# Choosing the tokens of each expert: one-hot products for two experts at once, 64 weights against 128 moving columns

## The reference

```python
n_tok = b * s                                  # 8192
k = n_tok // E                                 # E = 8 experts, 1024 tokens each
logits = xf @ Wr + br
Sm = jax.nn.softmax(logits, axis=-1)
G_t, idx_t = jax.lax.top_k(Sm.T, k)            # every expert takes its k best tokens
...
tokens = xf[idx]
...
mid = jax.nn.silu(jnp.einsum('keh,ehf->kef', tokens, Wu) + bu)
out = jnp.einsum('kef,efh->keh', mid, W_down) + b_down
y = jnp.zeros_like(xf).at[idx].add(G[..., None] * out)
```

## Time and profile before

| | us |
|---|---|
| median of three runs | 4523.12 |
| lowest and highest | 4513.47, 4530.17 |
| the profiled execution's own time | 4521.61 |
| its span in the trace | 4519.9 |
| TensorE busy (matmuls), share of the span | 3914.8, 87% |
| VectorE busy | 3019.1, 67% |
| first layer's `moe_choose`, softmax to `slots` | 78.3 to 178.5 |
| one-hot columns and products in it (L627 to L565) | 142.6 to 177.5 |

### The profile page before, as it was taken

The page is one execution under the profiler, slowest core; times in us unless marked ns, Lnnn a source line. Parts: engine busy times, 40 slices in busy tenths (PEclk is TensorE's granted clock), DMA queues, the critical chain, the costliest instruction groups (busy, mean ns, idle before and its releaser), DMA issues. The chain is left out here.

```text
span 4519.9 us, 137362 instructions
## 1 busy us (share of the span) xinstructions
PE 3914.8 (87%) x58832; PEld 2629.4 (58%) x58832; DVE 3019.1 (67%) x5402; ACT 2324.4 (51%) x3869; POOL 2358.8 (52%) x1536
## 2 busy tenths in 40 slices
PE   4599798999999996389979799699999999997799
PEld 2366454444444435256657444488878788886577
DVE  6411255888888866721156576699889899996575
ACT  2121142677777771112135477677776777773233
POOL 1154444222222224035433355599999999998454
PEclk7799898999999998689989899899999999998899
DMA  7333377655565637233232476633433343342662
GB/s 223 108 56 49 89 235 209 90 96 94 95 101 94 102 76 235 84 92 56 45 86 66 169 257 249 191 97 97 103 97 87 98 103 96 97 106 101 240 226 76
DMA packets 339380, 550.42 MB, mean 122 GB/s; under 512 B 55456, under 2 KB 238912, under 8 KB 338752
## 3 DMA queue, kind: packets, MB, share of 16 engines
q1 hardware_dynamic: 285264, 467.33, 39.0%
q0 software_dynamic: 24576, 34.10, 4.6%
q10 hardware_dynamic: 28912, 40.02, 2.5%
HBM read 335.56 MB, written 212.32 MB: 121 GB/s over the span
## 5 line engine op out<-in xcount | busy, mean ns | idle before, releaser
L2566 POOL TENSOR_TENSOR s_hc<-s_hs,s_ct 128x1024 f32<-128x1024 f32 x512 | 1202.2, 2393 | 64.6 <-DVE s_hs L2541 63.5
L2541 DVE TENSOR_TENSOR_SCAN s_hs<-s_hs,s_psB 128x1024 f32<-128x1024 f32 x512 | 1133.4, 2270 | 118.4 <-PE s_psB L2457 108.6
L2457 PE MATMUL s_psB<-s_diag,s_duT 128*32 128x128 f32 x32768 | 966.5, 274 | 63.4 <-issue 52.8
L2457 PEld LDWEIGHTS s_psB<-s_diag,s_duT 128*32 128x32 f32 x32768 | 925.2, 111 | 148.5 <-issue 116.8
L1380 DVE CUSTOM_DVE_ANT_0 a_masked<-a_psM,k_later 128x1024 f32<-128x1024 f32 (+7 forms) x1024 | 721.3, 750 | 132.7 <-PE a_psM L1439 116.5
L1362 ACT ACTIVATE a_wt<-a_psE 128x512 f32<-128x512 f32 (+1 forms) x1216 | 625.1, 579 | 258.2 <-PE a_psE L1470 253.7
L2396 ACT ACTIVATE s_hs<-s_dlt,s_aneg 128x1024 f32<-128x1024 f32 x512 | 586.5, 1146 | 272.9 <-POOL s_hc L2566 269.7
L1341 POOL TENSOR_SCALAR_AFFINE_SELECT a_wt<-a_wt 128x512 f32<-128x512 f32 x256 | 162.4, 635 | 673.8 <-ACT a_wt L1362 673.7
L1439 PE MATMUL a_psM<-a_kst,a_qst 96*32 96x512 bf16 (+3 forms) x4608 | 326.5, 336 | 27.0 <-DVE a_mx L1380 21.2
L1470 PE MATMUL a_psE<-a_qst,a_kst 99*32 99x512 bf16 (+3 forms) x4608 | 326.1, 332 | 12.7 <-ACT a_wt L1362 8.5
L2371 ACT ACTIVATE s_diag<-s_ident,s_bt 128x128 f32<-128x128 f32 x953 | 317.5, 388 | 24.1 <-ACT s_ys L2380 13.4
(11 more groups left out here) (368 smaller groups left out, 6268.3 us busy)
## 6 DMA issues: line engine op xcount, KB each, us to landing
s_dlt<-dd SPq DMA_DIRECT2D x128, 512.0 KB
a_qst<-qs SPq DMA_DIRECT2D x144, 128.0 KB, 6.1
a_kst<-ks SPq DMA_DIRECT2D x144, 128.0 KB, 6.7
yd<-s_ys ACTq DMA_DIRECT2D x33, 512.0 KB
vs<-a_va ACTq DMA_DIRECT2D x32, 512.0 KB, 3.6
zsd<-s_zs SPq DMA_DIRECT2D x32, 512.0 KB, 2.7
ucd<-s_uc SPq DMA_DIRECT2D x8, 2048.0 KB, 9.3
dd<-s_dl SPq DMA_DIRECT2D x32, 512.0 KB, 3.6
```

The lines of the kernel that those rows point to most:

```text
L2457: ins = pe.matmul(psB[s][DG * m:DG * (m + 1), c * P:(c + 1) * P], duT[j % 2][:, c, DG * r:DG * (r + 1)], diag[:, place(NB * g + m, u), c, ...
L2541: dve.tensor_tensor_scan(hs[k % RING][:, :], hs[k % RING][:, :], psB[s][:, :], 0.0, ALU.mult, ALU.add).then_inc(scanned, 1)
L2566: pool.tensor_tensor(hc[NB * (g % 2) + r][:, :], hs[k % RING][:, :], ct[:, g, :], ALU.mult).then_inc(weighed, 1)
```

## The change

Two experts, 2i and 2i + 1, share one product. The table of positions is laid out anew, so that the two lie 256 columns apart (the cast out of `psV` becomes two of 256 columns, and `constants` numbers `trow` to match). A weight load takes the 32 weights of both, 64 in all, and a matmul the 64 columns of both, 128 in all. Of the 64 x 128 results half are of use (weights and columns of the same expert), and the last step picks them out: `idx` keeps all 128 columns, and the turning (now L568) takes one expert of each pair at a time, by every second column of the identity.

The outputs fill 64 PSUM partitions, so two matmuls work side by side in two strips of 64, where four worked in strips of 32. Weight loads and matmuls go from 512 to 256 for each layer.

`H` is made in two parts again, but the first covers s = 0, 1, 2, three quarters of the tokens, by 64 instructions of 2 x 192 elements, and the second the rest, by 64 of 2 x 64.

```diff
@@ -472,11 +472,11 @@
         H = a.sb("H", [P, NH_, 512], bf16)
         hot = a.sb("hot", [P, NLO, 512], bf16)
         LW = a.sb("LW", [P, NLO, 2, 512], bf16)
-        idx = a.sb("idx", [P, 2, NH_])
+        idx = a.sb("idx", [P, 2, 2, NH_])
         idf = a.sb("idf", [P, E, 8])
         psV = a.ps("psV", [P, 4, P])
         psC = a.ps("psC", [P, 8])
-        psI, psI2 = a.ps("psI", [P, 8, NH_]), a.ps("psI2", [P, 8, NH_])
+        psI = [a.ps(f"psI{g}", [P, 4, P]) for g in range(2)]
         psO = a.ps("psO", [P, E, NLO, 2])
         shifted, exped = a.sem("shifted"), a.sem("exped")
         s_ready, s_stored = a.sem("s_ready"), a.sem("s_stored")
@@ -487,6 +487,7 @@
         lo_ready = a.sem("lo_ready")
         d_step, passed_on, inner_loaded = a.sem("d_step"), a.sem("passed_on"), a.sem("inner_loaded")
         STEPS = 30
+        PART = (0, 3)
         with nc.Block() as block:
             def regroup(eng, h):
@@ -545,25 +546,27 @@
                 pe.wait_ge(rows_ready, NLO // 4)
-                for half in range(2):
-                    pe.wait_ge(hot_ready, half + 1)
-                    for g in range(2):
-                        for k in range(TILES // 2):
-                            s, t = 2 * half + k % 2, k // 2
-                            for m in range(4):
-                                e = 4 * g + m
-                                col = (s * E + e) * 16 + t
-                                ins = pe.matmul((psI, psI2)[g][32 * m:32 * (m + 1), 0, :],
-                                                LW[:, :, :, col].rearrange("p v w -> p (v w)"), H[:, :, col],
-                                                start=(half == 0 and k == 0), stop=(half == 1 and k == TILES // 2 - 1))
+                for s in range(4):
+                    if s in PART:
+                        pe.wait_ge(hot_ready, PART.index(s) + 1)
+                    for t in range(16):
+                        for g in range(2):
+                            for m in range(2):
+                                col = 64 * s + 16 * (2 * g + m) + t
+                                pair = slice(col, col + 257, 256)
+                                ins = pe.matmul(psI[g][64 * m:64 * (m + 1), 0, :],
+                                                LW[:, :, :, pair].rearrange("p v w e -> p (v w e)"),
+                                                H[:, :, pair].rearrange("p v e -> p e v"),
+                                                start=(s == 0 and t == 0), stop=(s == 3 and t == 15))
                 ins.then_inc(idx_ps, 1)
                 pe.wait_ge(idx_copied, 2)
                 for g in range(2):
                     for u in range(2):
-                        ins = pe.matmul(psO[NH_ * u:NH_ * (u + 1), 4 * g:4 * (g + 1), :, :].rearrange("p e v w -> p (e v w)"),
-                                        idx[:, g, :], ident[:, :], start=True, stop=True)
+                        for odd in range(2):
+                            ins = pe.matmul(psO[NH_ * u:NH_ * (u + 1), 4 * g + odd:4 * g + odd + 3:2, :, :].rearrange("p e v w -> p e (v w)"),
+                                            idx[:, g, odd, :], ident[:, odd:P:2], start=True, stop=True)
                 ins.then_inc(out_ps, 1)
             @block.vector
@@ -618,7 +621,10 @@
                 dve.tensor_tensor(junk[:, :], junk[:, :], sg[:, :], ALU.add).then_inc(pos_ready, 1)
                 dve.wait_ge(posT_ready, 1)
-                link.step(dve.tensor_copy(posi[:, :], psV[:, :, :].rearrange("p s q -> p (s q)")))
+                for odd in range(2):
+                    link.inc(dve.tensor_copy(posi[:, 256 * odd:256 * (odd + 1)].rearrange("p (s t) -> p s t", t=16),
+                                             psV[:, :, :].rearrange("p s (e o t) -> p (s e) o t", o=2, t=16)[:, :, odd, :]))
+                link.wait()
                 link.inc(dve.tensor_scalar(hi_i[:, :], posi[:, :], NH_ - 1, None, ALU.bitwise_and))
                 link.step(dve.tensor_scalar(lo_i[:, :], posi[:, :], 6, None, ALU.logical_shift_right))
                 link.inc(dve.tensor_copy(hi[:, :], hi_i[:, :]))
@@ -630,14 +636,15 @@
                 for v in range(0, NLO, 4):
                     dve.tensor_tensor(LW[:, v:v + 4, 1, :], hot[:, v:v + 4, :],
                                       trow[:, :].rearrange("p (o c) -> p o c", o=1).to_broadcast([P, 4, 512]), ALU.mult)
-                for half in range(2):
-                    c = slice(256 * half, 256 * (half + 1))
+                for s, end in zip(PART, PART[1:] + (4,)):
+                    c = slice(64 * s, 64 * end)
                     for v in range(NH_):
-                        ins = dve.tensor_scalar(H[:, v, c], hi[:, c], float(v), None, ALU.is_equal)
+                        ins = dve.tensor_scalar(H[:, v, :].rearrange("p (o c) -> p o c", o=2)[:, :, c],
+                                                hi[:, :].rearrange("p (o c) -> p o c", o=2)[:, :, c], float(v), None, ALU.is_equal)
                     ins.then_inc(hot_ready, 1)
                 dve.wait_ge(idx_ps, 1)
                 for g in range(2):
-                    dve.tensor_copy(idx[:, g, :], (psI, psI2)[g][:, 0, :]).then_inc(idx_copied, 1)
+                    dve.tensor_copy(idx[:, g, :, :].rearrange("p e h -> p (e h)"), psI[g][:, 0, :]).then_inc(idx_copied, 1)
                 dve.wait_ge(out_ps, 1)
                 for u in range(2):
                     r, v = slice(NH_ * u, NH_ * (u + 1)), slice(8 * u, 8 * (u + 1))
@@ -2921,7 +2928,7 @@
     p = np.arange(P)
     same = (p[:, None] // 16 == p[None, :] // 16)
     col = np.arange(512)
-    s, c = col // (E * 16), col % 16
+    s, c = col % 256 // 64, col % 16
     return {
         "ident": np.eye(P, dtype=np.float32),
         "same16": same.astype(np.float32),
```

## The result

| us | before | changed |
|---|---|---|
| median (runs) | 4513.47 (9) | 4539.18 (9) |
| lowest, highest | 4505.82, 4530.17 | 4526.61, 4551.51 |
| span of the profiled execution | 4519.9 | 4537.9 |
| softmax to `slots`, layer 1, layer 2 | 99.7, 99.6 | 113.5, 113.5 |

The nine runs of the kernel before include the three of the forecast, whose median was 4523.12.

The account below looks back on a forecast made before the run. It took a chain with nothing beside it as the bound, VectorE's `H` and TensorE's products sharing the path. TensorE's end +15.4 and additions 0.4 made 15.8 us a layer, 31.6 for two, on 4523.1: 4555 us, range 4544 to 4566.

Parts of the forecast that it names:

- the step that decided it: TensorE's products: a strip fetches one scattered column each 1.70 to 1.97 ns, so products take 30.2 us, against 16.5 before.
- the rival of a slow pattern on VectorE: Making `H`: VectorE loses its fast rate on two stretches, first part 6.4 us later, total 4567 us; chance 0.05.
- the cast: The cast out of `psV`, split in two of 256 columns: 0.76 us back to back, +0.07.
- the copies: Copies to `idx` of 128 columns for 64: 284 against 219 ns each, +0.13 us.
- the wait for the second part: TensorE's wait for the rest of `H`: nothing, VectorE done at about 168.2, first three quarters of products until 184.
- a shared budget: Products: columns are the price but strips share one budget, rounds of 126 ns, +1.9 us a layer, 4527; chance 0.18.
- an instruction price: Products: instructions are the price, 31 ns a pair, some -4 us a layer, 4515, faster; chance 0.16.
- the limit is one of each strip's stream: Products: each strip fetches scattered columns for itself, 1.70 to 1.97 ns each, with no budget shared by four strips.
- its one load: First weight load of a burst, starting alone: 0.14 us against 0.10 contiguous, taken as evidence that strips share no budget.
- 17 ns beside its columns: Product round: time beyond column fetching, kept in the new round, 218 ns of columns making 235 ns.
- Turning: TensorE's turning before `slots`: 8 records in 0.66 us become 16 of 64 columns, 0 to +0.66, taken as +0.2.
- every us counts twice: Whole program: the stage's change moves everything after it, in both layers; 15.8 us a layer, 31.6 for two.

Follow-up runs that it names:

- the bursts: The kernel before with scratch products added in layer 1, varying widths, strips and spacing; two strips of 64 x 128 took 340 ns scattered, 56 contiguous.

## Why the prediction was right or wrong

Right: the direction, and the step that decided it. The rate of a strip's scattered columns is the price, at either clock, and pairing doubles the columns of each round while the rounds stay 128. In `H` the first part ended 2.1 us later (2.2 forecast) and the whole took 17.41 us (17.5), so the rival of a slow pattern on VectorE fell; the cast cost +0.07 and the copies +0.13, both as forecast; the wait for the second part cost nothing. The measured loads of 64 were 190 ns (187 forecast), single matmuls 399 (near 380). The rivals of a shared budget and of an instruction price fell, and not only in the total: each by a burst of its own.

Part of that was luck: *"the limit is one of each strip's stream"* holds only by how the columns lie. Four strips ran as if alone with their lines 16 to 64 bytes apart and queued at 2 or 256 bytes (212 and 224 ns for 97). In both kernels the strips read 32 bytes apart. The prediction did not look at that distance, and its one load could not have shown it.

Wrong, and by how much. Of 31.6 us forecast 20.3 were measured; of the 11.3 us between them, 3.9 lie in the stages and 7.4 outside them:
- *"the present round has 126 - 64 x 1.70 = 17 ns beside its columns, and I keep those."* In the stage this is the step that failed. The 17 ns were no fixed part of a round: they went with the place of the next weight load, which I read as the same bank as the moving columns, and the changed order no longer has it (the round before fell from 126 to 115 ns with the order alone). The round is 220 ns, all columns (128 x 1.72), not 235: 127 x 15 ns = 1.9 us a layer too many. With g outermost, as before the change, it is 249: neither order gives 235. I read the new loop order as neutral; it is worth 3.6 us.
- *Turning, 0 to +0.66, 0.2 taken.* It cost 0.08 (0.66 to 0.74), near the price by columns and far from that by count.
- *"So what this stage wins or loses moves everything after it [...]: every us counts twice."* This is the step that cost the forecast most, 7.4 us. 27.7 us were lost in the two stages, 20 (14 to 27) measured in the time, 16 and 27 on repeating. A kernel with a plain delay gave 28 and 33 for 28.5. So the rest of the program did not simply move in the changed kernel, or the scatter of its length hid that it did. The cause stays open. Between the stage and the total lie the parts whose clock varies from run to run; that source of error was named as scatter, not as a term.

With the stage right to the last tenth the forecast would still have been 4523 + 28 = 4551, or +0.6%, inside its range of 4544 to 4566. The measured ratio on its base of 4523.12 gives 4543.5, just below that range. The median itself is 4539.18, but the kernel before also had a median 9.65 us lower over nine runs than over the three. The measured +0.45% lies just inside the half per cent that a measurement can tell; the prediction gave 0.64 to lying beyond it and 0.35 to this side, and the repeats fell on both sides.

## What to carry to other kernels

Count the 16-byte lines that each column strip fetches, not the instructions. Merging two small products into one with twice the scattered operands doubled the lines of a strip, and half of what it fetched was of no use. Laying the columns side by side made the same product cheap (56 ns a round for 340 in the bursts). When operands must be strided, see to it that strips at work together read 16 to 64 bytes apart and not 0, 2, 256 or 512, and that a strip's next weight load lies 64 or 128 bytes away and not 2 or 256. A larger first part pays only if the consumer has been waiting for the second; here it waited 0.45 us and the later start cost 2.1.

## What the runs showed of the hardware

- One strip's moving stream takes 1.73 to 1.84 ns for each 16-byte line, at 1.2 and 2.4 GHz granted; full pace needed four 2-byte columns to a line (25.9 ns for 56 columns), two gave half of it (53.3).
- Four strips whose lines lie 16 to 64 bytes apart run as if alone (98 to 101 ns for 56 columns); at 0, 2, 256 or 512 bytes they queue (212 to 224), at 128 slightly (129).
- A weight load that follows its strip's moving columns at 2 or 256 bytes, and not 64 or 128, is longer, and so is the matmul: loads 147 against 138 ns for 32 weights and 218 against 190 for 64, matmuls 307 against 295 and 435 against 399. That a shared bank is the reason is inferred.
- With everything contiguous a pair of weight load and matmul (32 x 64) took 8.5 ns start to start in four strips.
